# Eight-expert FFN behind a LoRA FFN: Silu of even pairs later in ScalarE's queue, early expert ranks behind the last piece, next group's first splits behind the last sums

## What is computed

```python
# 2048 tokens (4 x 512 in the first part by adapters), H = 1024, F = 2752, rank 16, 8 experts, top 2
gate = x @ W_gate.T + 0.5 * (x @ A_gate[i].T) @ B_gate[i].T      # i: adapter of the sequence
up   = x @ W_up.T   + 0.5 * (x @ A_up[i].T) @ B_up[i].T
act  = silu(gate) * up
y    = act @ W_down.T + 0.5 * (act @ A_down[i].T) @ B_down[i].T
logits = y @ Wg + bg
top  = top_k(logits, 2)
z_e  = relu(y @ W_e[e] + b_e[e])                                 # experts e in top
out  = x + mean(z_e over the two experts of a token)
```

## Time and profile before

| | |
|---|---|
| median of 3 runs | 1881.9 us (1880.54 to 1886.08) |
| the profiled execution's own time | 1880.42 us |
| its span | 1878.6 us |
| TensorE busy | 1824.1 us (97%), mean granted clock 0.991 |
| VectorE busy | 1244.0 us (66%) |
| GpSimd busy | 1078.5 us (57%) |
| ScalarE busy | 742.6 us (40%) |
| DMA, mean | 186 GB/s |

### The profile page before, as it was taken

One profiled execution on the slowest core, in us unless ns is written; L12 is line 12 of the kernel. 1 busy time (PEld: TensorE's weight loads), 2 busy tenths in 40 slices (PEclk: granted clock), 3 DMA queues, 4 the chain that ended last, 5 costly groups with the idle time before them and its releaser, 6 DMA issues.

```text
span 1878.6 us, 24950 instructions
## 1 busy us (share of the span) xinstructions
PE 1824.1 (97%) x8583; PEld 1512.3 (81%) x8583; DVE 1244.0 (66%) x1500; ACT 742.6 (40%) x1054; POOL 1078.5 (57%) x643
## 2 busy tenths in 40 slices
PE   7999999999999999999999999999999999999997
PEld 6788888888888878887778888888877888888885
DVE  8877788875567787788878876477787542244400
ACT  5544444443543336433434444443322333333332
POOL 2678888873434454455555543444435666666664
PEclk9999999999999999999999999999998999999998
DMA  5556656745577655555565555577625875677643
GB/s 207 170 202 226 219 199 212 240 138 179 182 246 246 230 172 169 173 171 172 196 203 197 196 177 186 195 252 233 219 96 159 228 188 139 156 191 191 155 100 48
DMA packets 128395, 350.32 MB, mean 186 GB/s; under 512 B 15232, under 2 KB 17152, under 8 KB 128000
## 3 DMA queue, kind: packets, MB, share of 16 engines
q1 hardware_dynamic: 110320, 286.94, 44.8%
q0 software_dynamic: 17952, 61.75, 13.8%
HBM read 267.49 MB, written 90.05 MB: 190 GB/s over the span
## 4 chain that ended last, share of the span: by engine, by line
PE 75%; POOL 9%; DVE 6%; issue 5%; DMA 3%; ACT 1%; SPq 0%; POOLq 0%; ACTq 0%; DVEq 0%
PE PS L1680 23%; PE PS L1681 22%; PE PS L1682 22%; PE PS L1795 2%; PE PS L2018 2%; PE PS L1722 2%; DVE FT L1291 1%; POOL brw L748 1%; POOL FT L692 1%; POOL FT L687 1%; POOL FT L684 1%; DVE R L908 1%; POOL ytp L714 1%; DVE ring L889 1%; POOL FT L716 1%
## 5 line engine op out<-in xcount | busy, mean ns | idle before, releaser
L1680 PE MATMUL PS<-R,ring 128*128 128x512 f32 (+1 forms) x1800 | 710.6, 395 | 29.6 <-ACT FT L1114 12.6
L1681 PE MATMUL PS<-R,ring 128*128 128x512 f32 (+1 forms) x1800 | 704.5, 391 | 0.0
L1682 PE MATMUL PS<-R,ring 128*128 128x512 f32 (+1 forms) x1800 | 704.0, 391 | 0.0
L1680 PEld LDWEIGHTS PS<-R,ring 128*128 128x128 f32 x1800 | 340.1, 189 | 105.5 <-DVE ring L889 19.8
L1682 PEld LDWEIGHTS PS<-R,ring 128*128 128x128 f32 x1800 | 339.8, 189 | 72.3
L1681 PEld LDWEIGHTS PS<-R,ring 128*128 128x128 f32 x1800 | 340.3, 189 | 65.8
L769 POOL TENSOR_TENSOR ring<-raw,ring 128x1024 fp32r<-128x1024 f32 x78 | 192.7, 2470 | 268.2 <-ACT ring L895 268.2
L1680 PE MATMUL PS<-ring,R 128*128 128x512 f32 x592 | 232.3, 392 | 3.4 <-DVE FT L1236 3.4
L748 POOL DMA_INDIRECT brw<-in_bgu,idx_b x88 | 94.8, 1077 | 243.1 <-DVE R L1060 203.0
L1681 PE MATMUL PS<-ring,R 128*128 128x512 f32 x592 | 231.5, 391 | 0.0
L1682 PE MATMUL PS<-ring,R 128*128 128x512 f32 x592 | 231.2, 390 | 0.0
(11 more groups left out here) (191 smaller groups left out, 2353.9 us busy)
## 6 DMA issues: line engine op xcount, KB each, us to landing
raw<-in_wp SPq DMA_DIRECT2D x124, 512.0 KB
act_scratch<-FT SPq DMA_DIRECT2D x140, 256.0 KB, 5.1
FT<-act_scratch SPq DMA_DIRECT2D x70, 512.0 KB, 4.2
raw<-in_we SPq DMA_DIRECT2D x64, 512.0 KB
ytp<-in_wgb SPq DMA_DIRECT2D x96, 256.0 KB, 4.9
raw<-wt_scratch SPq DMA_DIRECT2D x40, 512.0 KB
out<-in_xn SPq DMA_DIRECT2D x17, 512.0 KB, 5.8
y_scratch<-FT SPq DMA_DIRECT2D x7, 1024.0 KB, 5.8
```

The lines of the kernel that those rows point to most:

```text
L1680: e.matmul(out_, hi, whi, start=start, stop=False, skip_group_check=True)
L1681: e.matmul(out_, hi, wlo, start=False, stop=False, skip_group_check=True)
L1682: return e.matmul(out_, lo, whi, start=False, stop=stop, skip_group_check=True)
```

## The change

Three things are moved; no operation is added or taken away.

1. The Silu of even units before the last gets a key 1.25 later.
2. Of group 1's first four `w_lo`, all go right behind the `d_add` of group 0's stage 6 (those have keys from `op(1, -1.95)`). Before, two stood ahead of these and two behind.
3. At the end of group 1, `early_ranks` goes from the middle of the last piece to the start of `last2`, `early_table` from behind the third remainder to behind the fourth, all four `lora2_out` ahead of the first `sum2`; and `early_hots` goes in VectorE's list behind the `d_add` of stage 6.

```diff
-                dve.add(key + 0.13, w_lo, g, n)
+                dve.add(op(1, -1.88 + 0.01 * n) if g and n < 4 else key + 0.13, w_lo, g, n)
...
-                        act.add(due + 0.35, silu, g, q, k)
+                        act.add(due + (1.6 if q < 20 else 0.35), silu, g, q, k)
...
-        dve.add(op_m(1, 36) + 2.31, early_hots)
+        dve.add(op_m(1, 38) + 0.2, early_hots)
         dve.add(op_m(1, 38) + 0.3, early_rows)
...
                 e.wait_ge(s_lp, g * NM + REM_M[6] + 1)
+                if g:
+                    early_ranks()
                 for i in range(4):
                     e.wait_ge(s_ev, ev_of(g, 6, i))
                     m = rem(g, 6, i)
                     if g and i < 2:
                         turn2(i)
-                    elif g and i == 2:
-                        early_table()
                 m.then_inc(s_pe, 2)
                 lora2_ready(g, 6)
-                if g == 0:
-                    for i in range(4):
-                        lora2_out(g, 6, i)
-                    return
-                e.wait_ge(s_ee, 3)
-                sum2(0)
-                turn2(2)
-                lora2_out(g, 6, 0)
-                sum2(1)
-                turn2(3)
-                lora2_out(g, 6, 1)
-                lora2_out(g, 6, 2)
-                sum2(2)
-                lora2_out(g, 6, 3)
+                if g:
+                    early_table()
+                for i in range(4):
+                    lora2_out(g, 6, i)
+                if g:
+                    turn2(2)
+                    e.wait_ge(s_ee, 3)
+                    sum2(0)
+                    sum2(1)
+                    turn2(3)
+                    sum2(2)
...
                         piece(g, s, kp)
-                        if g == NG - 1 and s == 6 and kp == 3:
-                            early_ranks()
```

## The result

The changed kernel takes 1862.78 us, the median of four runs (1861.63 to 1865.3); the kernel before takes 1881.22 beside it (four runs, 1878.87 to 1886.08). The ratio is 0.990 with a 95% interval of 0.9878 to 0.9923: 18.4 us less by the medians and 18.8 by the ratio, where 16.2 were forecast. The edits are numbered here as in the prediction: edit 1 is the Silu, edit 2 the tail of group 1 (third in the list of the change), edit 3 the first splits of group 1 (second there). The profiled execution took 1862.27 us, with a span of 1860.4.

The account below looks back on a forecast made before the run. TensorE, busy 97% of the span, was taken as the bound. Silu gains of 12.7 (group 1) and 1.3 (group 0), 1.9 for the group-change splits and 0.25 for the tail sum to 16.2 us: 1865.5 us, range 1859 to 1872.5.

Parts of the forecast that it names:

- the eight stalls: Group 1's pairs, before product 4: TensorE waits 1.44 us for a copy behind `silu(q,0)`; all eight go, 11.5 us.
- The wait near 951: Group 1, late sums let Silus hold a copy: of 1.49 us start to start, 0.65 stays and 0.83 goes.
- its own sign: Group 1: no wait of L1680 for the copy L1114 over 0.7 us would show the forecast right.
- `b_lo` has 0.7 us to spare: Inside group 1's pairs: adapter-row splits (L1060), the next wait for TensorE, would still be ready 0.7 us early.
- The ranks' wait: Tail of group 1: TensorE's 3.3 us wait for the mask before `early_ranks` goes.
- the new wait: Tail of group 1: TensorE waits 1.3 us at the early table for `early_hots`, in place of 3.3.
- By that row the fall comes near 1404.1: Tail: clock falls 3.2 us after the last `lora2_out`, the remaining 6.7 us double; last sum only 0.25 us earlier.
- B: Tail: small matmuls keep the clock at full rate, 7 us less, 1859 us; chance 0.11.
- C: Pairs: another wait, at `b_lo` or late sums, gives half the Silu gain back, 1872.5 us; chance 0.15.
- D: Pairs: the Silu's move does nothing because `c_add(q,0)` itself sets product 4's start, 1879.8 us; chance 0.05.
- E: Pairs: Silus over 16 us late for `gated` hold up VectorE; one us past gives 1899.7 us; chance 0.02.
- F: Clock falls early in the tail and the Silu move loses a little, 1869 to 1870 us; chance 0.02.

Follow-up runs that it names:

- silu_first: The kernel before with only the first Silu, `silu(q,0)`, of even units before the last keyed 1.25 later: 1872.82 us in a single run.
- silu_only: The kernel before with all four Silus of even units before the last keyed 1.25 later, nothing else changed: median 1870.86 us, ratio 0.9941 to before.
- a_later: The changed kernel with one `a_hi` split (L904) two steps later in ScalarE's queue, behind the last adapter rows: median 1862.21 us, ratio 0.9888 to before.
- silu_back: The changed kernel with the Silu's later key undone: median 1879.06 us, ratio 0.9979 to before.
- split_back: The changed kernel with the move of group 1's first `w_lo` splits undone: 1862.14 us in a single run.
- silu_latest: The changed kernel with the Silus of units 2 to 18 keyed 7.2 behind their sums' key instead of 1.6: 1861.74 us in a single run.
- silu_rest: The kernel before with only the other three Silus, not `silu(q,0)`, of even units before the last keyed 1.25 later: 1881.38 us in a single run.

## Why the prediction was right, and where it was off

**Edit 1: right in mechanism and place; right in size in part because two errors cancelled.** The forecast was 12.7 us in group 1; the leads give 16.48 - 3.61 = 12.87. silu_first shows that it is the Silu ahead of the copy and nothing else that makes the eight stalls. Each of them gave back 1.52 to 1.55 us and not 1.44: the prediction counted the late start but not that the matmul behind a wait is followed after 0.30 us instead of 0.23 (700.05 to 700.35, 941.69 to 942.00). That is 12.3 for 11.5. The wait near 951 gave less: a remainder of 0.65 and a gain of 0.83 were forecast; 0.85 stayed, 0.48 was gained (0.79 in silu_only), and 0.33 went again one product later, where the three Silus and two splits hold the next copy. The prediction asked whether the Silus come too late for `gated`, and not what they still stand ahead of. By its own sign (no such wait over 0.7 us) the 0.85 is a miss. Pairs of group 1 take 40.10 us, a little under the 40.3 to 40.5 it named. Group 0 gave 1.66 where 1.3 were forecast.

**The half unit at 1134** took 1.01 us of this trace's gain, which makes the net of edit 1 in group 1 11.9. The prediction put nothing here. The wait was found where the adapter rows stand in ScalarE's queue behind a split that waits for a DMA, and a_later shows that, since moving the split takes the wait away. But the 1.01 is no price of edit 1: the transfer took 7.21 us in this trace instead of 6.09, and three other traces with edit 1 lose nothing here. The expectation of silu_only, which counted it in, was wrong in that term. `b_lo` has 0.7 us to spare inside the pairs, as forecast: L1060 holds TensorE up once in the whole trace, and not in a pair.

**Edit 3: right.** 1.95 against 1.9; silu_back has 1.88, and split_back is 2.13 behind without it.

**Edit 2: right in its steps, off in one term.** The ranks' wait and the half-clock stretch went, the new wait is 1.33 against 1.3, the clock falls again. What failed is the step "By that row the fall comes near 1404.1": 17.3 us after step 3, from one row of the kernel before. It came at 20.4, so the last sum came 28.0 after step 3, 2.75 ahead of before, where 0.25 was forecast. That the sum had the right frame shows in the 24.0 us at full clock that the forecast implies (1410.8 - 1386.8), against 23.5 to 24.2 measured. The moment does not follow from this order alone: over five traces it varies by 5.6 us, worth 2.8 us at the last sum, and had silu_back's fall (16.2) come here, the term would have been about zero. So 0.25 was a possible value of a scattered term, and its mean in these traces is some 1.5 us. Why the moment scatters stays open. The leads say where forecast and result part, 16.2 against 18.45: 2.73 in the tail (18.45 - 15.47 = 2.98 for 0.25), 0.36 in group 0, 0.05 at the group change, and -0.84 in group 1. The last is the long transfer, so two scattered terms of opposite sign stand in the total; that it came within 2.3 us of the forecast is in part luck.

**The rivals.** B, that the clock does not fall: it falls in every kernel with sums alone. C, another wait gives half of edit 1 back: the nearest thing is the 0.33 us one product behind the wait near 951; the 1.01 at the half unit is a transfer's scatter. D, that the Silu's move does nothing: silu_only takes 11.1 us off by the ratio, and in the timeline the copy is over (761.57) before the sum begins (761.88). E, that the Silus come too late: silu_latest shows no loss with the Silus another 16 us late; where a loss begins was not tried. F had an early fall, at once behind the last `lora2_out`, and the fall came later than forecast.

## What to carry to other kernels

When an engine works in order, look for an instruction that waits while one behind it has its data: each such pair can cost the bound engine the difference every time it comes round, and moving the waiting one back costs little while its reader has slack. Then ask what the moved ones still stand ahead of when their own data are late: here they held the next copy once, for 0.33 us. When a wait appears in one trace at an irregular place, look at the same place in the other traces before calling it a price of the change: the 1.01 us at the half unit was one transfer's duration. Where a stretch of small matmuls sits near the clock's fall, give its cost as a span and not as one row's value: here it moved by 2.8 us between executions of the same order.

## What the runs showed of the hardware

- TensorE's clock falls to 0.50 (1.2 GHz) in stretches of 8-column sums and 128-column turns in which it is counted busy without a gap (7.60 of 7.60 us); in the one trace with 70 matmuls of 256 columns among them it stays at 1.00 (2.4 GHz).
- The moment of that fall differs between kernels whose TensorE program is the same there: 15.2, 16.0, 16.2, 20.4 and 20.8 us after the same matmul in five traces.
- A wait of 3.1 us costs more than itself: in silu_first 3.4 us at half clock follow it, 1.5 us more, as they do behind the 3.15 us wait for the mask in the earlier trace rows. Waits of 1.3 and 1.4 us in the pairs leave the clock at 1.00. Between them it is not settled: at the group change silu_first has 3.4 us at 0.50 from 700.7, behind a wait of 1.86 us, while waits of 1.76 to 2.05 at the same place leave the clock at 1.00 in before, silu_only, silu_rest and split_back.
- The same load of the stored activations (L904 waits for it) takes 6.0 to 7.2 us from issue to landing over the traces, and TensorE's loss at the half unit follows it.
- Behind the sums, between 47 and 56 us after step 3, there is a second fall in some executions; from the last sum to TensorE's last matmul it is 446.9 to 447.7 us with it and 444.7 to 444.9 without, 2.3 us. Two waits stand there, one for GpSimd (L806) and one of 1.81 us in every trace. Where the first is 1.25 us or more (eight traces) the clock falls; where it is 1.0 or less it falls in one of five, the kernel after. That wait is part of the 2.3 us, and what brings the fall on was not tried.
